# First loads on two queues and a new order of the work in a pipelined decoder layer

## The reference

```python
x = _layernorm(x + self_attn(x))                 # 16 heads of 16, causal
x = _layernorm(x + cross_attn(x, ctx_1024, mask))  # 375 keys for each sequence
x = _layernorm(x + fp4_ffn(x))                   # 256 -> 2 x 704 -> 256
```

## Time and profile before

| | |
|---|---|
| median of 3 runs | 662.46 us (661.29 to 663.10) |
| the profiled execution | 661.05 us |
| its span | 659.2 us |
| PE, DVE, ACT, POOL busy | 592.7, 509.9, 294.6, 213.8 us |
| ramp, to the first score product of slot 3 | 150.05 us |
| slots 3 to 13 | 391.74 us |
| drain | 117.41 us |

### The profile page before, as it was taken

One profiled execution on the slowest core, in us unless ns is written; L12 is line 12 of the kernel. 1 busy time (PEld: TensorE's weight loads), 2 busy tenths in 40 slices (PEclk: granted clock), 3 DMA queues, 4 the chain that ended last, 5 costly groups with the idle time before them and its releaser, 6 DMA issues.

```text
span 659.2 us, 16222 instructions
## 1 busy us (share of the span) xinstructions
PE 592.7 (90%) x5682; PEld 380.1 (58%) x5682; DVE 509.9 (77%) x1555; ACT 294.6 (45%) x717; POOL 213.8 (32%) x286
## 2 busy tenths in 40 slices
PE   3687798899999999999999999999999999997964
PEld 3445465566666666666666656665666665553532
DVE  3679688896978869696968687887969696979772
ACT  1144354445454555454545455454545454442411
POOL 5244234315150524242341515051424233223001
PEclk9789899899999999999999999999999999999996
DMA  6734461515252433526251525343342512120000
GB/s 168 212 95 138 140 191 49 175 32 150 75 152 86 132 107 74 164 56 178 54 143 59 158 70 151 87 133 106 91 148 59 173 50 88 49 88 2 9 7 14
DMA packets 64464, 67.78 MB, mean 103 GB/s; under 512 B 11696, under 2 KB 55936, under 8 KB 64384
## 3 DMA queue, kind: packets, MB, share of 16 engines
q1 hardware_dynamic: 64384, 66.75, 35.1%
HBM read 39.72 MB, written 27.00 MB: 101 GB/s over the span
## 4 chain that ended last, share of the span: by engine, by line
PE 64%; DVE 20%; issue 8%; ACT 3%; POOL 3%; SPq 1%; DMA 1%; DVEq 0%; POOLq 0%; ACTq 0%
PE misc L2020 18%; PE prob L1960 7%; PE misc L2101 6%; PE misc L2041 5%; PE xpv L2001 5%; PE misc L2012 5%; PE score L1946 5%; DVE junk L1262 4%; PE prob L1955 4%; DVE amax L1254 2%; PE apv L1989 2%; PE misc L2054 2%; PE misc L2062 2%; DVE qt L1176 2%; DVE hq L1180 1%
## 5 line engine op out<-in xcount | busy, mean ns | idle before, releaser
L1262 DVE CUSTOM_DVE_ANT_0 junk<-score,maskbias 112x375 bf16<-112x375 f32 x256 | 128.5, 540 | 43.3 <-PE score L1946 42.8
L800 ACT ACTIVATE xP<-prob 128x448 f32<-128x448 f32 (+1 forms) x192 | 98.5, 542 | 106.8 <-PE prob L1960 106.5
L638 POOL TENSOR_TENSOR rstd<-veps,half 112x1 f32<-112x1 f32 x48 | 27.2, 576 | 295.9 <-DVE veps L1340 295.9
L2020 PE MATMUL misc<-wguT,xqT 128*112 128x352 f32 x256 | 87.2, 468 | 0.5 <-ACT xqT L764 0.5
L633 POOL TENSOR_TENSOR move_a<-mT,negeye 16x448 bf16<-16x448 f32 x64 | 60.6, 969 | 77.9 <-ACT mT L764 77.9
L633 POOL TENSOR_TENSOR move_x<-mT,negeye 16x448 bf16<-16x448 f32 x64 | 65.3, 1036 | 53.9 <-ACT mT L764 53.9
L2020 PEld LDWEIGHTS misc<-wguT,xqT 128*112 128x112 f32 x256 | 44.2, 180 | 24.6 <-issue 2.9
L1960 PE MATMUL prob<-move_x,shift_x 128*128 128x448 bf16 x192 | 54.0, 360 | 1.5 <-POOL move_x L633 1.4
L2020 PE MATMUL misc<-xwvT_s,ctxT_s 128*128 128x256 f32 (+1 forms) x192 | 52.2, 395 | 0.0
L2101 PE MATMUL misc<-wdT,hqT 128*112 128x256 f32 x192 | 49.6, 402 | 1.5 <-ACT hqT L764 1.5
L1946 PE MATMUL score<-xK,xQ 64*128 64x375 f16 x256 | 42.9, 329 | 6.7 <-DVE xmax L1262 6.2
(11 more groups left out here) (163 smaller groups left out, 1117.5 us busy)
## 6 DMA issues: line engine op xcount, KB each, us to landing
xk_dram<-xk_parts SPq DMA_DIRECT2D x64, 192.0 KB, 3.1
xK<-xk_dram SPq DMA_DIRECT2D x16, 768.0 KB, 4.6
ctxT_s<-in_ctxT SPq DMA_DIRECT2D x16, 375.0 KB, 3.8
aq_dram<-aq_parts SPq DMA_DIRECT2D x64, 64.0 KB, 2.6
ak_dram<-ak_parts SPq DMA_DIRECT2D x64, 64.0 KB, 2.1
aQ<-aq_dram SPq DMA_DIRECT2D x16, 256.0 KB, 3.6
aK<-ak_dram SPq DMA_DIRECT2D x16, 256.0 KB, 2.8
xq_dram<-xq_parts SPq DMA_DIRECT2D x64, 64.0 KB, 2.1
```

The source lines that it names most:

```text
L800: act.activation(xP[0:KEYS[c], g % 2, c], prob[m][0:KEYS[c], 0:GH * S].rearrange("p (h q) -> p h q", h=GH), ACT.Exp).then_inc(probs.taken[ ...
L1262: dve.tensor_tensor_reduce(junk[:, m], score[m][0:S, 0:SC], maskbias[:], 1.0, -3.0e38, ALU.add, ALU.max, xmax[:, b.par, h:h + 1]).then_inc ...
L2020: mm = pe.matmul(misc[m][0:rows_, 0:cols], actT(c), weightT(c), start=(c == 0), stop=(c == DT - 1))
```

## The change

1. The four small loads of shift and gate are issued by ACT, at the head of its `prep`. SP begins with `wc_s`.
2. The loads of `woT`, the mask, `wgu` and x of batch 0 leave SP's `prep` and are placed one by one in its `ramp`, and the load of the three cross weights is split: `xwqT_s` gets its own semaphore `w_xq` and its own place.
3. The lists of steps of all five engines, and the misc ring's order with them, are new in `ramp`, `slot` and `drain`. What is computed, and the shape of each instruction, is the same.

```diff
@@ SP, prep and the new helpers
-                for t in range(DT):
-                    heads = slice(t * (P // HD), (t + 1) * (P // HD))
-                    sp.dma_start(shift_s[:, t, :], shift[heads, :].unsqueeze(1).to_broadcast([P // HD, HD, MS])).then_inc(w_mix, 16)
-                    sp.dma_start(gate_s[:, t:t + 1], gate[heads, :].unsqueeze(1).to_broadcast([P // HD, HD, 1])).then_inc(w_mix, 16)
                 sp.dma_start(wc_s[:], wc.rearrange("(t p) g -> p t g", p=P)).then_inc(w_mix, 16)
...
+            def load_wo():
                 sp.dma_start(woT_s[:], woT.rearrange("(t p) d -> p t d", p=P)).then_inc(w_wo, 16)
+            def load_mask():
                 sp.dma_start(mask_i, mask).then_inc(w_mask, 16)
                 sp.dma_start(mask_t_i[H:P, :], mask).then_inc(w_mask, 16)
-                load_x(Batch(0))
+            def load_wgu():
                 sp.dma_start(wgu_n[:], wgu.rearrange("(t p) d -> p t d", p=P)).then_inc(w_gu, 16)
-            def load_wx():
-                for dst, src in ((xwqT_s, xwqT), (xwkT_s, xwkT), (xwvT_s, xwvT)):
+            def load_wkv():
+                for dst, src in ((xwkT_s, xwkT), (xwvT_s, xwvT)):
                     sp.dma_start(dst[:], src.rearrange("(t p) d -> p t d", p=P)).then_inc(w_x, 16)
+            def load_wxq():
+                sp.dma_start(xwqT_s[:], xwqT.rearrange("(t p) d -> p t d", p=P)).then_inc(w_xq, 16)
@@ SP, start of ramp
+                load_wgu()
+                load_xT(Batch(1))
+                load_mask()
                 put_q(at[-2], at[0])
                 put_k(at[-2], at[0])
-                load_xT(Batch(1))
+                load_wo()
                 get(at[0], aq_dram, aQ, aq_out, aq_in, apv_done)
                 get(at[0], ak_dram, aK, ak_out, ak_in, apv_done)
-                next_xT(at[-1])
                 load_ctx(Batch(0))
-                load_wx()
-                next_ctx(at[-1])
+                load_wkv()
                 put_q(at[-1], at[1])
                 put_k(at[-1], at[1])
+                next_ctx(at[-1])
+                load_wxq()
...
+                load_x(Batch(0))
@@ ACT, prep
+                for t in range(DT):
+                    heads = slice(t * (P // HD), (t + 1) * (P // HD))
+                    act.dma_start(shift_s[:, t, :], shift[heads, :].unsqueeze(1).to_broadcast([P // HD, HD, MS])).then_inc(w_mix, 16)
+                    act.dma_start(gate_s[:, t:t + 1], gate[heads, :].unsqueeze(1).to_broadcast([P // HD, HD, 1])).then_inc(w_mix, 16)
                 act.wait_ge(w_mix, 16 * 7)
@@ misc ring, steady order
-MISC_ORDER = ["hT1", "hT0", "q", "down", "A.mT", "X.xT", "k", "gate0", "up0", "v", "gate1", "up1", "A.out",
-              "A.att", "K0", "A.o", "V0", "X.out", "K1", "X.att", "V2", "X.o", "A.xT", "X.mT", "V1", "A.q"]
+MISC_ORDER = ["hT1", "hT0", "q", "down", "A.mT", "X.xT", "k", "gate0", "up0", "gate1", "up1", "A.out", "v",
+              "A.att", "K0", "A.o", "V0", "X.out", "K1", "X.att", "V2", "X.o", "A.xT", "X.mT", "A.q", "V1"]
@@ POOL, slot
                 power(0, a)
+                shifts(0, a)
                 power(2, ft)
-                shifts(0, a)
-                shifts(2, ft)
-                keep_x1(a)
                 diagonal(i, c, 0, True)
                 diagonal(i, c, 1, True)
+                shifts(2, ft)
                 power(1, ct)
+                keep_x1(a)
                 diagonal(i, c, 2, True)
                 diagonal(i, c, 3, True)
@@ ACT, end of slot
-                layernorm(ft, 2, y[:, ft.par])
-                maxima(i, 1, "X.mT")
-                ctxv(i, kv, 1)
-                xq_hi_(i, a)
+                maxima(i, 1, "X.mT")
+                xq_hi_(i, a)
+                ctxv(i, kv, 1)
+                layernorm(ft, 2, y[:, ft.par])
@@ PE, the semaphore of the cross query weights, and the drain around down of batch 13
+            def project_q(i, b):
+                if b.c == 0:
+                    pe.wait_ge(w_xq, 16)
+                    pe.nop(nofuse=True)
+                project(i, "A.q", xwqT_s, x1T, S, after=("A.xT",))
...
                 pv_cross(at[16], at[15], 0, 1)
+                turned_cross(at[16], at[15], 0, 2)
+                down(at[16], at[13])
...
                 turn_out(at[16], at[15], "X.out", xoT, xoT_ready)
-                down(at[16], at[13])
                 turn_att(at[16], "X", 1)
```

More of the change, by code:

```diff
@@ L711, in slot @@
                 diagonal(i, a, 0, False)
+                residual(a)
                 diagonal(i, a, 1, False)
@@ L1753, in drain @@
[L1753 to L1762 removed]
+                quant_h(at[15], at[13], 0, 5)
@@ new lines, in drain @@
+                max_cross(at[15], at[15], 3)
+                residual_ffn(at[15], at[12])
+                max_cross(at[15], at[15], 4)
+                quant_h(at[15], at[13], 1, 2)
+                max_cross(at[15], at[15], 5)
+                moments(at[15], at[12], 2, "down", 0)
+                max_cross(at[15], at[15], 6)
+                quant_h(at[15], at[13], 1, 3)
+                max_cross(at[15], at[15], 7)
+                quant_h(at[15], at[13], 1, 4)
+                normalise(at[15], at[14], 1, "X.out", 0)
@@ L2385, in drain @@
                 turned_cross(at[15], at[14], 0, 1)
+                turn_hq(at[15], at[12], "hT0", range(4))
+                turn_xq(at[15], at[13])
+                turned_cross(at[15], at[14], 0, 2)
+                gate_up(at[15], at[13], "gate", 0)
+                gate_up(at[15], at[13], "up", 0)
+                gate_up(at[15], at[13], "gate", 1)
+                gate_up(at[15], at[13], "up", 1)
+                down(at[15], at[12])
+                scores_cross(at[15], at[15], 0)
                 pv_cross(at[15], at[14], 0, 0)
-                turned_cross(at[15], at[14], 0, 2)
```

909 lines of the change are left out of this document (444 added, 465 removed), and 18 rows, old and new, of tables (MISC_IN, MISC_OUT).

## The result

The changed kernel took **657.36 us** (median of 6 runs, 656.83 to 660.78), the kernel before 663.22 on the same chip (6 runs, 661.29 to 665.74). The ratio is 0.9912, with a 95% interval of 0.9894 to 0.9931: 5.9 us faster. The profiled executions have 657.26 and 661.05 us, 3.8 apart; the kernel before had a good one, 2.2 us under its own median.

A forecast was written before the change was run, and what follows sets the result against it. PE was taken to bound the slots, with more to win in the ramp. 661.05 -5 (ramp) +0 (slots) -1 (drain) = 655.05; with two thirds of the median's 1.41 excess, 656.0 us, range 648.5 to 663.

The forecast's parts named there:

- The head, -1.65: Kernel start: with small loads on ACT's queue, the last gate load lands 1.65 us earlier, and all that follows with it.
- Rival 4: Head: the small loads land as late from ACT's queue beside the large ones, 657.6 us; chance 0.07.
- First scores, -2.3: Ramp: put_k starts where put_q ends, so batch 0's first scores come about 2.3 us earlier, near 24.8.
- Ramp, -5: Stage before the equal slots: -6.4 at the first cross scores and +1.9 make -4.5, taken as -5 us; bounds -8 and -1.65.
- +1.9 "given back": Ramp: four fewer weight quantisation steps done on DVE when X.mT of batch 0 comes, costing 1.9 us.
- Rival 2: Ramp: DVE's quantisation bounds the fill, so only 0 to 2 us remain, 659.5 to 661.5; chance 0.18.
- Slots, 0: Eleven equal slots: X.mT wait stays, amax wait goes (-1.9), small losses against it; sum 0, bounds -7 and +4.4 us.
- Rival 1: Slots: DVE is late at X.mT or the hq transposes, 0.9 us a slot, +9.9, so 666 us; chance 0.11.
- rival 3: Slots: both recurring waits go, giving 649 us; chance 0.11.
- Drain, -1: Final stage: -1.5 for the earlier down product, +0.5 for work that must find holes; bounds -3 and +2 us.
- -1.5 for down: Drain: batch 13's down product no longer stands ahead of the attention output's transpose, saving 1.5 us.
- The clock, "no change": Ramp: PE still idles some 5 us ahead of the first scores, so its clock falls again, costed at no change.

The follow-up runs named there:

- quiet_head: drain_before with SyncE holding the first xT and later loads until the seven mixing loads landed, and the second xT ahead of wgu: 651.30 us.
- early_ctx: drain_before with woT and the first ctxT loaded ahead of the first q and k exchange, xwkT and xwvT one exchange later: 651.28 us.
- slot_alone: The kernel before with only the change's slots (slot orders of all five engines and the slot's bank order): 656.68 us.
- drain_before: The changed kernel with the drain of the kernel before (all five engines' orders and the bank order there): 650.80 us.
- down_later: The changed kernel with batch 13's down product moved behind the turning of the last cross attention's output: 660.86 us.
- quiet_early: drain_before with the edits of both quiet_head and early_ctx: 650.98 us.

## Why the prediction was right or wrong

The time was forecast at 656.0 (648.5 to 663) and came out at 657.36; faster, with 0.74. The mechanism was right in part, and luck did the rest: against the profiled executions the ramp's term was off by +0.8, the slots' by -3.3 and the drain's by +4.8, and these errors cancel.

- **The head, -1.65: failed.** The mixing product is 0.15 us later (10.47 to 10.69 over eight executions, 10.52 before). The step at fault reads the DMA share of 0.09 between 3 and 4 us as room for the gate load. That share was low because the small loads stood ahead of the large ones; with the large ones issued first, it is 0.88 in the same microsecond. quiet_head shows 0.9 us at the mixing product when they are held. The Trainium skill's "DMA: Bandwidth & Descriptors", section "Issuing engines are not separate DMA queues", had this right: the queues interleave on the same DMA engines, only issue time is saved. Rival 4 (0.07) is what the head did, though its 657.6 us agrees with the measured time only because other terms erred too.
- **First scores, -2.3: failed, +1.2.** put_k does start where put_q ends, but put_q, forecast at 15.2 with the head's gain, went out at 17.05, so put_k came at 19.82: 0.34 us sooner, not 2.35. And "from there to the scores it is 6.95 us as before" is wrong: from put_k's issue at 19.82 it is 8.5 us (7.7 to 9.0 over eight executions), since aK lands beside woT, ctxT, xwkT and xwvT. early_ctx, with these moved, has 7.2.
- **Ramp, -5: right in size, wrong in its steps.** A.mT of slot 0 came 2.3 us earlier and not 6.3, the cross scores 1.8 and not 6.4. The +1.9 "given back" to VectorE's quantising did not come: the lead grows instead, to 2.9 us at X.mT of batch 0 (75.94 instead of 78.84; 0.8 to 3.7 over eight executions) and 4.17 at slot 3. One wait that went is the 1.68 us for x1 of slot 2 (at 110.21 before; 0.20 at 105.86 now). Over eight executions the same ramp ends 2.1 to 5.4 us earlier than the earlier trace rows have it. Rival 2, the ramp bound by VectorE at 0 to 2 us, did not happen.
- **Slots, 0: mis-sized, -3.3** (within the bounds of -7 and +4.4). The amax wait went as forecast. The X.mT wait, which "stays", went too: the turning of x1 ahead of it waits for ScalarE in its place. The two waits are not where the gain stands: the idle time rose by 3.2 us over the eleven slots, and the modelled busy time fell by 6.5. Several groups of products are 0.5 to 1.1 us shorter in sum (context V, self PV, the hq transposes), and no run shows why; slot_alone shows only that the slot's own order brings the gain. Rival 1 (slots lose 0.9 each) did not happen; of rival 3 both waits went, but others took their place, and its price of 7 did not come.
- **Drain, -1: failed, +3.8,** outside its bounds of -3 and +2; against the old order behind the same slots it is +6.5 (121.19 to 114.68). The step saw the place ("FFN 13 before the last scores, and DVE then is the limit for ten microseconds") and gave it 0.5 us as so much work looking for holes. It did not follow what stands behind it: the chain of batch 14 through X.out, X.o and quantisation, whose xq comes 3.6 us later than in the kernel before and 5.4 later than in drain_before. Nor did it have a term for the clock, at 0.50 for ten us after TensorE had idled for over a third of the ten before. Which of the two costs how much stays open. The -1.5 for down was also wrong in kind: down_later shows the product filling a wait for VectorE.
- **The clock, "no change": failed, both ways.** It did fall again at the hole ahead of the first scores, but came back some us sooner: 0.78 (up to 0.98 in the same ramp) between 30 and 40 us instead of 0.55, and 0.54 in slot_alone with the old ramp. By these rows (0.23 to 0.43 of ten us) that is 2.3 to 4.3 us of full clock, an estimate, and so a likely source of the lead at A.mT in spite of the late scores; no run parts it from the order. In the drain it fell, where the sum had no term for it.

## What to carry to other kernels

A low DMA share beside a small load says nothing about the share once the large loads are issued ahead of it: price a load by what will be in flight with it. A gain at an early mark of a fill need not reach its end: 2.7 us at the first scores (quiet_early) were no gain in the time. When a new order moves a block of one stage in front of a wait, follow every chain that runs behind it to the end of the program, not the work's total, and test the stages apart: here two gained and one lost, and putting the old drain behind the new ramp and slots was worth more than the whole change (650.8 us against 657.4, from 663.4).
